# One Sigmoid in place of Exp, Ln, Exp, and the copy of psO moved down VectorE's order, in a gated layer on eight cores

## What is computed

```python
x = L0_attn_x                                   # (2, 16384, 1024)
xn = (x - mean(x)) / sqrt(var(x) + 1e-5)
B = xn @ W2 + b2;  C = xn @ W3 + b3             # 16 columns each
delta = softplus(xn @ W1 + b1)
s = sum over n of C[n] * xn * delta * B[n]      # = xn * delta * dot(B, C)
xh = xn @ H                                     # Hadamard, 1024 x 1024
scale = max(max|xh|, 1e-5) / 7
xq = clip(round(xh / scale), -8, 7) * scale
wq = ternary(weight) * mean|weight| per row
out = x + s * silu(xq @ wq.T)
```

## Time and profile before

| | |
|---|---|
| time, median of 2 runs | 592.99 us (592.79 to 593.19) |
| profiled execution: its time, and the span of its slowest core (core 1) | 593.89 us, 592.4 us |
| spans of the eight cores | 589.4 to 592.4 us |
| mean granted TensorE clock | 0.820 to 0.828 of full speed |
| busy, share of the span | PE 64%, DVE 52%, ACT 58%, POOL 43% |
| DVE idle in front of o3s, waiting for POOL's ob | 162.4 us in 30 waits, the longest 5.8 |
| chain that ended last, by engine | DVE 46%, POOL 25%, issue 10%, PE 8%, DMA 5% |

### The profile page before, as it was taken

How to read it: one execution, slowest core, us unless ns; L and a number is a source line. 1 busy time by engine, 2 the same in 40 slices (tenths; PEclk the granted TensorE clock), 3 DMA queues, 4 the chain that set the end, 5 groups by cost and what they waited for, 6 DMA issues and landing times.

```text
span 592.4 us, 7129 instructions; the slowest of 8 cores (589.4 to 592.4 us)
## 1 busy us (share of the span) xinstructions
PE 381.5 (64%) x1696; PEld 157.8 (27%) x1696; DVE 305.4 (52%) x632; ACT 344.0 (58%) x393; POOL 255.0 (43%) x183
## 2 busy tenths in 40 slices
PE   0041436987777777787878777778777767977300
PEld 0011213433223233232333323223232323423100
DVE  1438883555555455555555555555555554444540
ACT  1603315898666666666667777667666665655520
POOL 5001420214444555555554444444444455564374
PEclk9996576998778888888887878778787878979765
DMA  7982202346433333334435353333433222211201
GB/s 132 220 245 95 83 18 71 73 101 131 107 99 94 95 98 96 108 107 107 107 106 108 96 82 106 101 98 106 108 106 108 71 71 72 71 55 55 87 35 71
DMA packets 80972, 57.77 MB, mean 98 GB/s; under 512 B 70435, under 2 KB 70564, under 8 KB 80932
## 3 DMA queue, kind: packets, MB, share of 16 engines
q1 hardware_dynamic: 72916, 34.19, 26.0%
q0 software_dynamic: 8016, 23.14, 11.9%
HBM read 25.93 MB, written 16.78 MB: 72 GB/s over the span
## 4 chain that ended last, share of the span: by engine, by line
DVE 46%; POOL 25%; issue 10%; PE 8%; DMA 5%; DVEq 2%; ACT 1%; SPq 1%; POOLq 1%; ACTq 0%
POOL ob L33 12%; POOL t4b L33 12%; DVE t3b L33 7%; DVE t1b L33 6%; DVE o3s L33 6%; DVE mx L33 6%; DVE xsm L33 5%; DMA xnT<-xnb 3%; DVE tbf L33 2%; DMA xb<-x 2%; DVEq L32 2%; DVE absum L33 2%; DVE msq L33 2%; PE psZ L264 1%; PE psZ L265 1%
## 5 line engine op out<-in xcount | busy, mean ns | idle before, releaser
L33 POOL TENSOR_TENSOR t4b<-t3b,o3s 128x1024 f32<-128x1024 f32 x32 | 75.2, 2350 | 209.1 <-DVE t3b L33 209.1
L308 PE MATMUL psXH<-Hs,uT 128*128 128x512 bf16 x128 | 73.1, 571 | 98.2 <-ACT xqm L33 96.1
L33 DVE COPY o3s<-psO 128x1024 f32<-128x1024 f32 x32 | 39.2, 1225 | 162.6 <-POOL ob L33 162.4
L264 PE MATMUL psZ<-W1c,xnT 128*128 128x512 bf16 x256 | 109.1, 426 | 0.5 <-DVE bcw L33 0.5
L265 PE MATMUL psZ<-W1c,xnT 128*128 128x512 bf16 x256 | 106.5, 416 | 0.0
L285 PE MATMUL psO<-ternT,xqT 128*128 128x512 bf16 x256 | 98.5, 385 | 11.1 <-ACT s L33 11.1
L33 ACT ACTIVATE xqm<-psXH,c_s,inv 128x1024 bf16<-128x1024 f32 x32 | 38.5, 1205 | 106.3 <-DVE cc L33 106.0
L286 PE MATMUL psO<-ternT,xqT 128*128 128x512 bf16 x256 | 98.1, 383 | 0.0
L33 POOL TENSOR_TENSOR ob<-xb,t4b 128x1024 f32<-128x1024 f32 x32 | 76.0, 2373 | 4.6
L310 PE MATMUL psXH<-Hs,vT 128*128 128x512 bf16 x128 | 74.1, 579 | 0.0
L33 ACT ACTIVATE esb<-psZ 128x1024 f32<-128x1024 f32 x32 | 32.8, 1024 | 47.5 <-PE psZ L267 46.4
(11 more groups left out here) (53 smaller groups left out, 480.7 us busy)
## 6 DMA issues: line engine op xcount, KB each, us to landing
xb<-x SPq DMA_DIRECT2D x32, 512.0 KB, 4.1
out<-ob POOLq DMA_DIRECT2D x32, 512.0 KB, 3.0
wfst<-wf POOLq DMA_DIRECT2D x8, 512.0 KB, 3.6
W1c<-w POOLq DMA_DIRECT2D x8, 256.0 KB, 18.9
Hs<-hpk SPq DMA_DIRECT2D x1, 512.0 KB
xnT<-xnb SPq DMA_TRANSPOSE x32, 3.1
xqT<-xqb SPq DMA_TRANSPOSE x32, 3.1
W23s<-w POOLq DMA_DIRECT2D x1, 64.0 KB, 3.9
```

The lines of the kernel that those rows point to most:

```text
L33: inst = fn(*a, **kw)
L264: pe.matmul(psZ1[:, 0:512], lh, W1c[ic][:, 0:512], start=(ic == 0), stop=False)
L308: pe.matmul(psXH[:, 0:512], uT2[t % 4][:, ic * 128:(ic + 1) * 128], Hs[:, ic * 512:(ic + 1) * 512], start=(ic == 0), stop=(ic == 3))
```

## The change

The three activations become one, `Sigmoid`, which reads psO with the scale `sa` and writes `s` directly. `nsa` (the negated scale) is gone, and `sa` gets four buffers in place of two, since the activation reads it two turns after it was written. The copy `o3s` stands further down in DVE's turn: behind `dot`, ahead of `t1b`. What it waits for, and what waits for it, is unchanged.

```diff
-        rs = mk1("rs"); nmrs = mk1("nmrs"); sa = mk1("sa"); nsa = mk4("nsa")
+        rs = mk1("rs"); nmrs = mk1("nmrs"); sa = mk4("sa")
...
                     ac.wait_ge(sO3S, w_ + 1)
-                    ac.activation(esb[:], psO3x[w_ % 2][:], AF.Exp, scale=nsa[w_ % 4][:])
-                    ac.activation(l2[:], esb[:], AF.Ln, bias=1.0)
-                    ac.activation(s2[w_ % 3][:], l2[:], AF.Exp, scale=-1.0, _inc=(sSIG, w_ + 1))
+                    ac.activation(s2[w_ % 3][:], psO3x[w_ % 2][:], AF.Sigmoid,
+                                  scale=sa[w_ % 4][:], _inc=(sSIG, w_ + 1))
...
-                w_ = c - 3
-                if 0 <= w_ < nt:
-                    dv.wait_ge(sPEO3, w_ + 1)
-                    if w_ >= 2:
-                        dv.wait_ge(sVOUT, w_ - 1)
-                    dv.tensor_copy(o3s[w_ % 2][:], psO3x[w_ % 2][:], _inc=(sO3S, w_ + 1))
                 u = c - 1
                 if 0 <= u < nt:
...
-                    dv.tensor_single_scalar(nsa[u % 4][:], sa[u % 2][:], -1.0, ALU.mult)
...
                     dv.tensor_reduce(dot[td % 2][:], prod[:], AX.X, ALU.add)
 
+                w_ = c - 3
+                if 0 <= w_ < nt:
+                    dv.wait_ge(sPEO3, w_ + 1)
+                    if w_ >= 2:
+                        dv.wait_ge(sVOUT, w_ - 1)
+                    dv.tensor_copy(o3s[w_ % 2][:], psO3x[w_ % 2][:], _inc=(sO3S, w_ + 1))
                 w2 = c - 4
```

More of the change, by code:

```diff
@@ L404, in _ @@
                     dv.tensor_single_scalar(mxc[:], mx[:], 1e-5, ALU.max)
-                    dv.tensor_single_scalar(sa[u % 2][:], mxc[:], 1.0 / 7.0, ALU.mult)
-                    dv.tensor_single_scalar(nsa[u % 4][:], sa[u % 2][:], -1.0, ALU.mult)
-                    dv.reciprocal(inv[u % 2][:], sa[u % 2][:])
-                    dv.tensor_tensor(cc[u % 4][:], dot[u % 2][:], sa[u % 2][:], ALU.mult, _inc=(sMX, u + 1))
+                    dv.tensor_single_scalar(sa[u % 4][:], mxc[:], 1.0 / 7.0, ALU.mult)
+                    dv.reciprocal(inv[u % 2][:], sa[u % 4][:])
+                    dv.tensor_tensor(cc[u % 4][:], dot[u % 2][:], sa[u % 4][:], ALU.mult, _inc=(sMX, u + 1))
                 v4 = c + 4
```

## The result

| | before | changed |
|---|---|---|
| median | 593.21 us (8 runs) | 518.97 us (9 runs, 518.77 to 520.25) |
| ratio, 95% interval | | 0.874 (0.872 to 0.877) |
| profiled execution: time, span of its slowest core | 593.89, 592.4 (core 1) | 520.25, 518.6 (core 4) |
| mean granted TensorE clock, by core | 0.820 to 0.828 | 0.867 to 0.886 |
| busy, share of the span: PE, DVE, ACT, POOL | 64, 52, 58, 43% | 67, 65, 67, 49% |

The forecast was 511 us, in a range from 496 to 534. The whole gain is 74 us.

The account below looks back on a forecast made before the run. The prediction took DVE and POOL waiting for each other as the bound, 15.49 us a tile. E (esb) of turn 4 at 126.9, 24 turns of 12.3, three of 10.3, and the end gave 511 us, range 496 to 534.

Parts of the forecast that it names:

- the ring over POOL and the o3s in front of mx: DVE and POOL wait for each other: 15.49 us a tile, 5.40 of it DVE's wait at o3s for ob.
- DVE with POOL at 11.3 to 11.9: Turn of DVE and POOL after the move, in us; the upper end if prod is caught by uT.
- The table loads at 1.28, without a drain: ACT: two uncovered loads a full turn, 57 more in all, making ACT's turn 11.76 us.
- The path over two turns: From o3s through ACT and PE to the next o3s: 22.8 to 23.9 us, so 11.4 to 12.0 a turn.
- The size of the turn: Full pipeline, esb to esb: 12.3 us, from 11.9 with one turn in three slow by 1.2; between 11.8 and 13.2.
- The last three steps: Steps to turn 31 without new tiles for ACT: PE's 9.75 and the o3s path rule, 10.3 us each, 31 together.
- Start and end: esb of turn 4 at 126.9 us; after the esb of turn 31, 56.9 us in place of 56.4.
- A drain (566 us): Rival: each ACT table switch costs a drain too, up to 1.24 us more; turn of 14.2 us; chance 0.10.
- a fetch from memory (656 us): Rival: each ACT table switch fetches from memory, 4.1 us in place of 1.28; turn of 17.4 us; chance 0.03.
- PE would be slow in every turn (13.2): Rival: PE at low clock throughout, 13.2 us a turn, 532 us; upper end of the forecast case, no separate chance.
- DVE and POOL wouldn't meet: Rival: DVE and POOL don't disturb each other, loads partly hidden or skipped; turn 11.3 us or less, 484 us; chance 0.05.
- DVE would simply wait elsewhere: Rival: the move brings nothing because DVE would wait in front of mx; counted within the range, no separate chance.

Follow-up runs that it names:

- the filling: Changed kernel plus eight unused 512-column PE matmuls ahead of psXH in each of turns 2 to 30: 505.26 us, ratio 0.851.
- the fastest kernel: Kernel before (three activations kept) with o3s moved between nmrs and bcw, and cc, msq, prod each reading one SBUF tensor: 486.15 us, ratio 0.819.
- the run without table loads: Changed kernel with Exp in place of Sigmoid, so the gate is no longer the layer's: 499.92 us, ratio 0.844.
- the run with one operand: Changed kernel with cc, msq and prod rewritten so that each reads only one tensor out of SBUF: 512.74 us, ratio 0.864.

## Why the prediction was right

**What bounded the kernel** was the ring over POOL and the o3s in front of mx. The move alone took 80 us off, Sigmoid alone 6.

**DVE with POOL at 11.3 to 11.9.** The upper end was it: 11.96 where nothing else held the turn, with each step within 0.2 us of the working, and prod caught by uT, which the working had left open. Taking the second SBUF operand away showed the reason.

**The table loads at 1.28, without a drain.** 1283 ns each and 0.01 or 0.02 us to the activation behind, in 58 cases. So the upper bound (1.24 more for each) was not reached. The drain of about 1380 ns that the Trainium skill gives ("ScalarE: Activation LUTs", "What ACT_TABLE_LOAD costs") isn't in this trace; its 1283 ns for the load are. That each activation here has already waited for the one ahead of it is the reason that the prediction gave for this, and no run tests it. The loads aren't hidden: without them the kernel is 19 us faster. ACT's turn with them was put at 11.76 and measured at 11.73.

**The path over two turns.** That it counts was shown by o3s ahead of bcw, which took 15 us from the run with the move alone. That its long turns come from PE's clock was shown by the filling, and Sigmoid in the fastest kernel showed that the same falls of the clock lengthen no turn once o3s is out of that path.

**The size of the turn: 12.62, not 12.3.** This is the term that was too small. Starting from 11.9, I took one turn in three slow at 1.2 us, a choice between two bounds for which there was no row. In the changed kernel the clock fell in every second one, 12 of the 24 turns from 4 to 28, and since two turns took 25.24 us on the mean, each fall cost 25.24 - 2 x 11.9 = 1.4 us. PE's wait at psXH was 1.97 or 1.98 us where it can be read; I had counted with 2.1, between the 1.73 and the 3.65 of the earlier trace rows, and couldn't tell what the clock would do behind it. Against the forecast it is 0.32 x 24 = 7.7 us.

**The last three steps: 34.5 us, not 31.** From 428.50 to 463.01. I left one thing out: once there is no new tile, lnv is gone, and the second load stands in front of esb, behind its wait for psZ, so it adds to PE's 9.75 and isn't beside it. The waits of ACT's loads for psZ (6.7 us in all, in the group above) are those turns. ACT's timeline:

```profile
450.69 1.28 ACT L33 ACT_TABLE_LOAD   x1 [2.50 <-PE psZ L267]
451.98 1.02 ACT L33 ACTIVATE esb<-psZ 128x1024 f32<-128x1024 f32 x1
...
461.72 1.28 ACT L33 ACT_TABLE_LOAD   x1 [1.58 <-PE psZ L267]
463.01 1.02 ACT L33 ACTIVATE esb<-psZ 128x1024 f32<-128x1024 f32 x1
```

The last two steps are 11.03 = 9.75 + 1.28 each. The run with the move alone has no loads there, and its three steps took 30.7 us.

**Start and end.** esb of turn 4 came at 125.6, put at 126.9. After the last esb there are 55.6 us, put at 56.9. Together with the two terms above: -1.3 + 7.7 + 3.5 - 1.3 = 8.6, and 510.0 of the working is 518.6 of the span.

**The rivals.** A drain (566 us) and a fetch from memory (656 us) were excluded by the 58 loads. That PE would be slow in every turn (13.2) was refuted as argued: the long turn leaves PE no wait. That DVE and POOL wouldn't meet fell with cc, msq and prod at three times their length. That DVE would simply wait elsewhere came true in part: its wait for line 301 in front of bcw grew from 25.1 to 62.3 us, and not the one in front of mx that I had looked at (3.9 us for psXH in all). It is the path over two turns that makes it wait there.

## What to carry to other kernels

In an in-order engine that waits on another one, look at what is queued behind the wait and doesn't need it: here 6 us of DVE's work a turn stood behind one copy, and where exactly the copy goes mattered again (behind dot 513 us, ahead of bcw 498). Fewer instructions on an engine are not a gain when they bring table loads: one Sigmoid and two loads took 0.26 us more than the three activations that share a table. When several limits lie within half a microsecond, sum each of them, also over two turns, and ask which of them a lower clock or a held-up instruction would lengthen.

## What the runs showed of the hardware that I had not expected

What PE's clock did after a wait in front of psXH, in turns of about 12 us, is not told by the length of the wait alone. In the changed kernel cores 0 and 1 have 28 waits of 1.97 or 1.98 us in the turns from 4 to 28; behind 23 of them the clock fell to 1.2 GHz, behind 5 it stayed. Two of them, from core 0:

```profile
229.19 0.38 PE L308 MATMUL psXH<-Hs,uT 128*128 128x512 bf16 x1 [1.98 <-ACT xqm L33]
...
266.34 0.58 PE L308 MATMUL psXH<-Hs,uT 128*128 128x512 bf16 x1 [1.98 <-ACT xqm L33]
```

In the fastest kernel the waits are 1.73 us in nearly every turn, 2.01 at the longest, and the clock stays up; its PE timeline:

```profile
288.97 0.38 PE L308 MATMUL psXH<-Hs,uT 128*128 128x512 bf16 x1 [1.73 <-ACT xqm L33]
```

In the run without table loads the wait is 1.98 us in 13 turns; after 6 of them the clock stayed, after 7 it fell:

```profile
209.53 0.38 PE L308 MATMUL psXH<-Hs,uT 128*128 128x512 bf16 x1 [1.98 <-ACT xqm L33]
...
221.48 0.52 PE L308 MATMUL psXH<-Hs,uT 128*128 128x512 bf16 x1 [1.98 <-ACT xqm L33]
```

What besides the length decides it stays open here. Filling 1.7 us of PE's wait with matmuls of no use held the clock up in every turn from 3 on and made the changed kernel 2.6% faster.

The second thing the prediction had supposed from two rows, and the run with one operand made it certain. Even the smallest of DVE's instructions, a product of two columns of one value for each row, is held up by a running POOL instruction for as long as that one lasts, if both its operands come out of SBUF as tensors (msq 654 ns on the mean); the same product with the second operand as a one-column scalar isn't (214 ns), and neither is prod with one operand out of PSUM (175 ns, 620 before).
